# Post-norm transformer block on one core: the last batch's attention in two query blocks, pairwise stack transfers, silu through tanh

## The chip, the core and the metric

One NeuronCore of a Trainium2 chip. The metric is device time in microseconds of one launch. The engines are PE (matmul), DVE (VectorE), ACT (ScalarE), POOL (GpSimd) and SP, which here only issues DMAs. Every engine runs its own list of instructions in order and meets the others only at semaphores.

## What is computed

x is 4 batches x 512 tokens x 128 features, fp32; 16 heads of 8 features; the hidden width is 512.

```python
qkv = einsum('bnd,ed->bne', x, qkv_w) + qkv_b      # per head q, k, v of 8
attn = softmax(q @ k.T * 8**-0.5)                  # 16 heads, 512 x 512
x = layernorm(x + (attn @ v) @ fc_w.T + fc_b + x)
h = silu(tlin(x, w1)) * tlin(x, w2)                # tlin: matmul with a ternary weight, times a scale
h = gelu(tlin(h, h1)); h = gelu(tlin(h, h2))       # exact gelu
x = layernorm(x + tlin(h, w3))
```

## The kernel before

**Orders by hand.** `SP_ORDER`, `PE_ORDER`, `ACT_ORDER`, `DVE_ORDER` and `POOL_ORDER` (L8 to L66) are lists of tokens. `walk` (L264) yields them with a running number, and each engine's loop turns a token into instructions with its waits. In PE_ORDER `S:5` also says in which of the 8 PSUM banks the result goes; `until_free` waits until the bank's last reader is done.

**Attention.** q and k are split in three bf16 parts each (`parts`, tokens `q`, `r`, `mid`, `lo`, `da`, `db`), six slots of part products per head. `spread` and `first_spread` (`zq`, `zk`, L343) copy them by DMA to `stack[0]` (q) and `stack[1]` (k), one DMA of 48 KB per head and side: even heads in partitions 0 to 63, odd heads in 64 to 127. So one bf16 matmul of 64 rows gives exact scores. `S` makes the scores of 128 queries x 512 keys, `s` on DVE takes the negated row maximum (L803). When all `S` of a group (mostly 4 heads) are through, `m` on POOL splits the maxima in three bf16 parts, PE transposes them, ACT copies them to `mT` and `mrow` puts them by two DMAs into three more rows of the stack. `T` repeats the score matmul transposed (128 keys x 512 queries) with the maximum already subtracted, `e` on ACT is the exponential (L654) into one of 16 `prob` buffers, and `P` multiplies four heads' probabilities with V (and a column of ones for the sum), 32 columns of the array for each head. `S` runs some 30 tiles ahead of `T`. After two P groups: `o` (copy to SBUF, transpose), `or`, `om` (reciprocal, normalise), `a` (transpose of the result), `f` (output projection), `l1` with five steps (add, statistics, aggregate, add of eps, result) and POOL's power `p1` between the fourth and the fifth.

**MLP**, in float32r with each activation in a high and a low part. `X` transposes x1, `Xh`/`Xl` split it; `A` and `B` are the two gates, 4 blocks each; `t` and `u` on ACT, `t` on DVE, `u` on POOL form the gate; `h0`/`l0` split it; `H` are the pieces of the hidden layers (4 output blocks x 4 input blocks, two matmuls each, the high and low part), `h` copies, `g` is a gelu over all four blocks, `gh`/`gl` split the result; `W`, `w3`, `Y`, `l2` (with POOL's `p2`), `out`. The weights' low parts are tested for zero once (`L`), and are zero, so each product takes one weight.

**Units.** `UNITS` are what goes through the MLP at once: batches 0, 1, 2 whole (512 columns) and batch 3 as two halves of 256. The attention of batch 3 runs whole, so both halves begin their MLP after the last `P`. For them silu is ACT's Silu (`ws`) and the rest of the gate and all splits are DVE's; up to batch 2's first hidden layer the splits are POOL's. `K` on PE are four filler matmuls of a zero tile.

**Weights.** h1 is loaded at the start, h2 and w3 (`lh`, `l3` in SP_ORDER) behind the stack transfers of batch 0; `wt` transposes them, `wc`/`wl` on POOL split them.

## Time and profile before

| | |
|---|---|
| median of 3 runs | 324.12 us (322.74 to 324.79) |
| span of the profiled execution, first to last instruction | 320.4 us |
| instructions in it | 5569 |
| matmul records, DVE, ACT, POOL instructions | 1804, 516, 433, 227 |
| row maxima on DVE, exponentials on ACT | 256, 256 |
| DMAs `stack<-parts`, 48 KB each | 124 from SP, 4 from ACT |

The profile is one execution. Its span is 3.7 us under the median. "Busy" is the time in which at least one instruction of an engine is under way; matmuls are pipelined, so for PE it is not work. A record's duration holds its latency, so that instructions of one engine start closer together than their durations say.

### The profile page before, as it was taken

The page shows a single profiled execution, that of the slowest core. Times are in us where ns is not written, and L with a number is a line of the kernel's source. Part 1 is how long each engine was busy: PE and PEld are TensorE (multiplying, and loading weights), DVE is VectorE, ACT ScalarE, POOL GpSimd, SP SyncE. Part 2 cuts the span into 40 slices and gives each one's busy share as a digit, 9 for nine tenths or more (in the row PEclk, how much of TensorE's full clock was granted, in tenths as well). Part 3 has the DMA queues.
Part 4 walks back from the last instruction along what each step waited for, and adds up shares of the span by engine and source line. Part 5 has one row for each costly group of instructions (what it writes and reads, how often), then busy time and mean ns, then how long its engine had stood idle before and what let it go on. Part 6 is the DMA issues. An engine that isn't in the chain of part 4 may idle for free.

```text
span 320.4 us, 5569 instructions
## 1 busy us (share of the span) xinstructions
PE 295.8 (92%) x1804; PEld 138.5 (43%) x1804; DVE 244.1 (76%) x516; ACT 234.8 (73%) x433; POOL 148.8 (46%) x227
## 2 busy tenths in 40 slices
PE   8567998999997999999999999999999999999991
PEld 6421132422332344334544233625634353579990
DVE  3959899998989899998996859298684410289883
ACT  3562567999683896898688998697799989447340
POOL 6762038651043793118807778063478913610201
PEclk9985899999999899999999999999999999999996
DMA  5643353313211321212030023310100010000101
...
DMA packets 17830, 13.44 MB, mean 42 GB/s; under 512 B 2551, under 2 KB 16648, under 8 KB 17800
## 3 DMA queue, kind: packets, MB, share of 16 engines
...
## 4 chain that ended last, share of the span: by engine, by line
PE 60%; ACT 11%; DVE 9%; POOL 8%; issue 6%; DMA 4%; SPq 1%; ACTq 1%; POOLq 0%; DVEq 0%
PE bank L445 26%; PE bank L480 11%; PE bank L465 9%; PE bank L456 6%; DVE negmax L803 6%; ACT prob L654 4%; DMA h_nat<-in_L_ffn_h_w_dram 3%; PE bank L420 2%; ACT L654 2%; POOL hT L990 2%; POOL parts L960 2%; PE bank L531 1%; ACT h_nat L729 1%; PE bank L438 1%; PE bank L503 1%
## 5 line engine op out<-in xcount | busy, mean ns | idle before, releaser
L803 DVE TENSOR_REDUCE negmax<-bank 128x1 f32<-128x512 f32 x256 | 160.2, 682 | 23.0 <-PE bank L456 22.5
L654 ACT ACTIVATE prob<-bank 128x512 f32<-128x512 f32 x256 | 136.7, 604 | 29.0 <-PE bank L465 27.4
L480 PE MATMUL bank<-prob,v_sb 128*32 128x512 f32 x512 | 73.0, 608 | 0.4 <-ACT prob L654 0.3
L456 PE MATMUL bank<-stack 61*128 61x512 bf16 x256 | 65.9, 398 | 4.3 <-DMA stack<-parts 2.6
L445 PE MATMUL bank<-act,hT 128*128 128x512 f32 (+1 forms) x320 | 68.3, 359 | 0.1
L465 PE MATMUL bank<-stack 64*128 64x512 bf16 x256 | 61.4, 389 | 2.2 <-DVE negmax L803 1.0
L445 PEld LDWEIGHTS bank<-act,hT 128*128 128x128 f32 x320 | 49.2, 190 | 14.3 <-issue 6.4
L722 ACT ACTIVATE h_nat<-bank,hs_all 128x512 f32<-128x512 f32 (+1 forms) x40 | 22.8, 603 | 22.4 <-PE bank L445 22.4
L456 PEld LDWEIGHTS bank<-stack 61*128 61x128 bf16 x256 | 17.6, 94 | 49.7 <-issue 26.9
L978 POOL CAST mparts<-negmax 128x16 bf16<-128x16 f32 (+1 forms) x17 | 3.7, 219 | 74.3 <-DVE negmax L803 74.3
L465 PEld LDWEIGHTS bank<-stack 64*128 64x128 bf16 x256 | 14.0, 94 | 51.0 <-issue 36.2
L954 POOL TENSOR_TENSOR rstd<-rstd,mhalf 128x4 f32<-128x4 f32 (+1 forms) x10 | 10.1, 1006 | 35.1 <-DVE rstd L784 35.1
L1028 POOL TENSOR_TENSOR act<-h_nat,act 128x512 fp32r<-128x512 f32 x20 | 25.4, 1274 | 1.3
L1023 POOL CAST act<-h_nat 128x512 fp32r<-128x512 f32 x20 | 12.1, 610 | 19.1 <-ACT h_nat L729 19.1
L480 PEld LDWEIGHTS bank<-prob,v_sb 128*32 128x32 f32 x512 | 10.7, 108 | 21.1 <-issue 17.2
L445 PE MATMUL bank<-x1T,w12T 128*128 128x512 f32 (+1 forms) x80 | 18.4, 372 | 0.4 <-DVE x1T L858 0.4
L840 DVE RECIPROCAL rden<-bank 128x32 f32<-128x32 f32 x8 | 2.8, 351 | 18.3 <-PE bank L420 18.3
L1013 POOL TENSOR_TENSOR act<-work,act 128x512 fp32r<-128x512 f32 x12 | 15.2, 1278 | 0.7
L1002 POOL TENSOR_TENSOR work<-work 128x512 f32<-128x512 f32 x12 | 15.2, 1282 | 0.4 <-ACT work L712 0.3
L445 PEld LDWEIGHTS bank<-x1T,w12T 128*128 128x128 f32 x80 | 12.7, 195 | 4.9 <-issue 2.0
L960 POOL COPY parts<-parts 128x512 bf16<-128x512 bf16 x12 | 7.9, 693 | 8.6 <-ACT parts L666 8.6
L427 PE MATMUL bank<-wz 128*128 128x128 bf16 x97 | 9.8, 245 | 1.4 <-DVE wz L752 1.0
(120 smaller groups left out, 343.0 us busy)
## 6 DMA issues: line engine op xcount, KB each, us to landing
stack<-parts SPq DMA_DIRECT2D x124, 48.0 KB
...
h_nat<-in_L_ffn_h_w_dram SPq DMA_DIRECT2D x1, 1024.0 KB, 8.1
work<-in_L_ffn_h_w_dram SPq DMA_DIRECT2D x1, 1024.0 KB, 5.6
...
stack<-mT SPq DMA_DIRECT2D x30, 6.0 KB
```

Source lines behind the costliest of these rows:

```text
L445: mm = nc.tensor.matmul(dst, w, v, start=first and n == 0, stop=last and n == len(pairs) - 1)
L456: nc.tensor.matmul(space("S", n)[:, :], stack[0][half_of(h, MROW), h // 2, qt * P:(qt + 1) * P], stack[1][half_of(h, MROW), h // 2, :], st ...
L465: nc.tensor.matmul(space("T", n)[:, :], stack[1][half_of(h, TR), h // 2, kt * P:(kt + 1) * P], stack[0][half_of(h, TR), h // 2, :], start= ...
L480: last = nc.tensor.matmul(space("P", pfirst)[at:at + VW, :], v_sb[b % 2][:, kt, of:of + VW], prob[:, t % NP, :], start=kt == 0 and slot % ...
L654: nc.scalar.activation(prob[:, n % NP, :], space("T", n)[:, :], ACT.Exp, scale=SCALE).then_inc(emptied("T", n), 1)
L722: nc.scalar.activation(raw[:, k, cols(u)], space(*h_first(u, layer, k))[:, 0:width(u)], ACT.Gelu if direct(u, layer) else ACT.Copy, scale= ...
L803: nc.vector.tensor_reduce(negmax[:, g % 2, col:col + 1], space("S", n)[:, :], AX.X, ALU.max, negate=True).then_inc(emptied("S", n), 1)
L960: nc.gpsimd.tensor_copy(parts[i][:, a, :], parts[i][:, 0, :])
L1002: nc.gpsimd.tensor_tensor(gate[:, k, cols(u)], gate[:, k, cols(u)], up[:, n % 2, cols(u)], ALU.mult).then_inc(gate_ok, 1)
L1013: nc.gpsimd.tensor_tensor(a[1][:, k, cols(u)], gate[:, k, cols(u)], a[0][:, k, cols(u)].bitcast(F32), ALU.subtract).then_inc(lo0, 1)
L1023: nc.gpsimd.tensor_copy(acts[u][layer + 1][0][:, k, cols(u)], raw[:, k, cols(u)]).then_inc(hi_g, 1)
L1028: nc.gpsimd.tensor_tensor(a[1][:, k, cols(u)], raw[:, k, cols(u)], a[0][:, k, cols(u)].bitcast(F32), ALU.subtract).then_inc(lo_g, 1)
```

## The change

- **Units and groups.** The attention of batch 3 is done for queries 0 to 255 and then for 256 to 511 (units 3 and 4), in groups of 8 heads. A `T` tile of them is two matmuls of 256 columns for two key blocks in one bank, and a `P` step is two sets of four matmuls of 256 columns. o, a, f, l1 and the MLP run per unit, so that unit 3's can stand among unit 4's attention in the orders.
- **Stack.** `parts` has eight slots. Slot 6 and 7 hold zeros (q) and ones (k), set once, instead of memsets of the whole stacks. One DMA of 128 rows fills a pair of heads on one side, and one DMA (two in units 3 and 4) brings a group's maxima, now four rows per head. The head order in V and in `om` is plain; v is four, om two smaller instructions instead of two and one.
- **Silu** is tanh on ACT and a product on DVE in all units (`hs12` scales), as it was in batches 0 to 2.
- **Who splits.** POOL now also splits batch 2's second hidden layer, unit 3's gate and unit 3's first hidden layer; DVE splits unit 3's second and all of unit 4's. Unit 3's first hidden layer has the wide gelu, the second and unit 4's have gelus per block.
- **Orders.** All five are new. SP issues `more`, `l3` and the second `lh` ahead of the first stack transfers, ACT issues no DMAs. `K`, `ws` and `wg` are gone.

The core of the diff:

```diff
-lw lh xin vb zq*4 zk*6 zq mrow zq*3 lh l3 xin mrow more xres xin spread mrow spread mrow spread mrow spread mrow spread xres mrow spread mrow spread
-mrow spread mrow*2 spread xres mrow spread mrow spread out spread mrow xres mrow*2 out*4
-"""
+lw lh xin vb
+more l3 lh zq zk*2 zq*2 xin zq*2 zk*3 zq zk*3 mrow zq*2 mrow xres mrow*2 spread*2 xin mrow spread mrow spread mrow xres spread mrow spread mrow spread
+mrow spread mrow*2 xres spread*3 mrow spread mrow*2 xres out mrow*2 out*4"""
...
-H:0 H*3 f:6 H:7 H*3 H:5 H*3 X:4 K:0 X:3 W:1 W A:2 B:0 A:6 B:7 A:5 B:4 A:2 B:3 A:6 B:0 A:5 B:7 A:2 B:4 A:6 B:5 W*2 H:3206 H*4 Y:7 H*5 H:4157 H*9 H:3206
-H*9 H:4157 H*9 W:3 W*3 K:0 W:2 W Y:0 W K:1 W K:0 Y:6
...
+W:0 W T:2 T:7 T:3 T:5 W*2 P*3 Y:4 H:1 o:2 H*3 H:7 H*3 H:3 H a:5 H*2 H:0 H*3 f:6 X:4 H:2 A:5 A:1 A:7 A:3 B:0 B:6 B:4 B:5 H*3 H:1 H*3 H:0 H*3 H:6 H*2
+W:2 H H:7410 H W H W*2 H*6 Y:3 H H:6527 H*9 W:4 W*3 Y:1"""
...
-h e*3 h e g e*5 wg o a*2 h*4 ws t*8 wg w3 h*16 w3*2
+h e h e*2 h m h g o e*3 a e*3 m e*14 t u t*3 w3 u*2 e*4 o u e*8 o a h*3 m h g t u*2 t*3 e*12 u h e u h e*3 m h*2 g o e*16 w3 o a h*4 g t*4 h*4 w3 h*8
+w3"""
...
+s*2 t*4 l2*2 s*3 or om s*2 l2 s*3 or om s*5 l1*5 l2*2 s Xh s Xl s*6 t s*2 t*3 s*4 or om l2*2 or om l2*4 l1*5 Xh Xl t*2 gt*2 h0 l0 t gh gt h0 l0 gl gh
+h0 gh t gl*2 gh gl gt h0 l0*2 gh gl gh*3 gl*3 l2*3 gh gl gh*2 gl gh gl*2 l2*7"""
...
+p1 gl*2 xr u h0 l0 u*3 h0*2 l0 h0 l0*2 m p1 p2 gh*2 gl gh gl gh gl*2 u*2 m u gh*4 gl*4 u h0*3 l0*2 h0 l0*2 p2 p1 gh*2 gl gh*2 gl*3 p2*2"""
...
-    GROUPS = [(0, 0, 2), (0, 2, 2)] + [(b, GH * j, GH) for b in range(B) for j in range(NG) if b or j]
-    UNITS = [(b, 0, NT) for b in range(LAST)] + [(LAST, t0, 2) for t0 in (0, 2)]
+    UNITS = [(0, 0, NT), (1, 0, NT), (2, 0, NT), (3, 0, 2), (3, 2, 2)]
+    NU = len(UNITS)
+    GROUPS = [(0, 0, 2), (0, 2, 2), (0, 4, 4), (0, 8, 4), (0, 12, 4), (1, 0, 4), (1, 4, 4), (1, 8, 4), (1, 12, 4), (2, 0, 4), (2, 4,
+              4), (2, 8, 4), (2, 12, 4), (3, 0, 8), (3, 8, 8), (4, 0, 8), (4, 8, 8)]
+    GATE_DVE = {4}
+    SPLIT0 = [0, 0, 0, 0, 1]
+    SPLIT_G = [(0, 0), (0, 0), (0, 0), (0, 1), (1, 1)]
+    DIRECT = {(3, 1), (4, 0), (4, 1)}
+    INNER_K = {4}
...
+        def spread(eng, i, p, done):
+
+            eng.dma_start(stack[i][:, p, :], parts[i][2 * HD * p:2 * HD * (p + 1), :, :]).then_inc(done, 16)
 
...
-                    for e in range(2):
-                        sp.dma_start(stack[0][TR * e + MROW:TR * e + TR, s0 // 2:(s0 + ns) // 2, :],
-                                     mT[rows * e:rows * (e + 1), 0:P]).then_inc(mrow[n % NG], 16)
+                    each = m_dmas(n)
+                    rows, to = m_rows(n) // each, nt // each
+                    for d in range(each):
+                        sp.dma_start(stack[0][MROW:P:MSTEP, s0 // 2:(s0 + ns) // 2, (t0 + to * d) * P:(t0 + to * (d + 1)) * P],
+                                     mT[rows * d:rows * (d + 1), :]).then_inc(mrow[n % NG], 16)
...
+                    w, each = width(u), N // width(u)
+                    for c in range(each):
+                        kt = each * k + c
+                        last = nc.tensor.matmul(space("T", n)[:, c * w:(c + 1) * w], stack[1][half_of(h), h // 2, kt * P:(kt + 1) * P],
+                                                stack[0][half_of(h), h // 2, cols(u)], start=True, stop=True)
+                    last.then_inc(ps_st, 1)
...
+                    for c in range(each):
+                        for t in range(t0, t0 + nh):
+                            _, k, slot = T_TILES[t]
+                            kt, at, of = each * k + c, VW * (slot % GH), VC * slot
+                            last = nc.tensor.matmul(space("P", pfirst)[at:at + VW, 0:w], v_sb[b % 2][:, kt, of:of + VW],
+                                                    prob[:, t % NP, c * w:(c + 1) * w],
+                                                    start=kt == 0 and slot % (GH * PO) < GH, stop=kt == NT - 1 and slot % (GH * PO) >= GH)
...
-                    if u < LT:
-                        nc.scalar.activation(gate[:, k, cols(u)], space("A", n)[:, 0:width(u)], ACT.Tanh, scale=hs12[:, 0, k:k + 1]).then_inc(ev_w1, 1)
-                    else:
-                        nc.scalar.activation(gate[:, k, cols(u)], space("A", n)[:, 0:width(u)], ACT.Silu, scale=hs[:, 0, k:k + 1]).then_inc(emptied("A", n), 1)
+                    if BEFORE[u]:
+                        until_0(act, lo0, BEFORE[u] - 1, k)
+                    nc.scalar.activation(gate[:, k, cols(u)], space("A", n)[:, 0:width(u)], ACT.Tanh, scale=hs12[:, 0, k:k + 1]).then_inc(ev_w1, 1)
...
-            def k_ones(j):
-                nc.vector.memset(stack[1][:, 2 * j:2 * j + 2, :].rearrange("p h n -> p (h n)").bitcast(F32), TWO_ONES).then_inc(ones, 1)
-
             nc.vector.memset(wz[:, :], 0.0).then_inc(wz_ok, 1)
-            for j in range(NG):
-                k_ones(j)
+            nc.vector.memset(parts[1][:, 6:8, :].rearrange("p m n -> p (m n)").bitcast(F32), TWO_ONES).then_inc(ones, 1)
...
 
-            for j in range(NG):
-                nc.gpsimd.memset(stack[0][:, 2 * j:2 * j + 2, :].rearrange("p h n -> p (h n)").bitcast(F32), 0.0).then_inc(zeros, 1)
+            nc.gpsimd.memset(parts[0][:, 6:8, :].rearrange("p m n -> p (m n)").bitcast(F32), 0.0).then_inc(zeros, 1)
+            nc.gpsimd.memset(mparts[:, :].bitcast(F32), 0.0).then_inc(parts_z, 1)
```

## Rows read from the trace of the kernel before

**Rows 1.** The page, busy time, share and instructions of each engine

```profile
PE 295.8 (92%) x1804; PEld 138.5 (43%) x1804; DVE 244.1 (76%) x516; ACT 234.8 (73%) x433; POOL 148.8 (46%) x227
```

**Rows 2.** Busy by stretch: PE, PEld, DVE, ACT, POOL, then clock, DMA share, GB/s

```profile
20.00:40.00 20.00, 17.22 (x61) 3.44 (x62) 18.46 (x31) 10.27 (x26) 5.63 (x13) 0.66 0.36 64
...
18.70:120.00 101.30, 93.01 (x521) 29.38 (x522) 93.52 (x168) 74.70 (x155) 47.55 (x79) 0.92 0.30 60
120.00:274.80 154.80, 153.27 (x917) 65.33 (x916) 106.49 (x212) 133.09 (x227) 82.02 (x117) 1.00 0.13 25
274.80:320.40 45.60, 37.62 (x284) 33.88 (x280) 32.89 (x116) 18.84 (x40) 7.52 (x8) 0.94 0.05 14
```

**Rows 3.** Groups by line and form: busy us, mean ns, idle before

```profile
L803 DVE TENSOR_REDUCE negmax<-bank 128x1 f32<-128x512 f32 x256 | 160.2, 682 | 23.0 <-PE bank L456 22.5
L722 ACT ACTIVATE h_nat<-bank,hs_all 128x512 f32<-128x512 f32 x24 | 16.5, 688 | 13.4 <-PE bank L445 13.4
L722 ACT ACTIVATE h_nat<-bank,hs_all 128x256 f32<-128x256 f32 x16 | 6.3, 475 | 8.9 <-PE bank L445 8.9
L729 ACT ACTIVATE h_nat<-h_nat 128x2048 f32<-128x2048 f32 x5 | 9.6, 1911 | 0.1
L729 ACT ACT_TABLE_LOAD x5 | 6.4, 1283 | 0.2
L1028 POOL TENSOR_TENSOR act<-h_nat,act 128x512 fp32r<-128x512 f32 x20 | 25.4, 1274 | 1.3
L1023 POOL CAST act<-h_nat 128x512 fp32r<-128x512 f32 x20 | 12.1, 610 | 19.1 <-ACT h_nat L729 19.1
```

**Rows 4.** Timeline of PE: start, duration, then what, with its count

```profile
129.92 1.07 PE L480 MATMUL bank<-prob,v_sb 128*32 128x512 f32 x8
130.91 0.39 PE L456 MATMUL bank<-stack 61*128 61x512 bf16 x2
...
135.62 1.20 PE L445 MATMUL bank<-act,hT 128*128 128x512 f32 x4
136.75 0.39 PE L465 MATMUL bank<-stack 64*128 64x512 bf16 x1
...
292.31 1.09 PE L445 MATMUL bank<-act,w3T 128*128 128x512 f32 x4
293.24 2.56 PE L445 MATMUL bank<-act,hT 128*128 128x256 f32 x20
```

**Rows 5.** Timeline at the start of the tail

```profile
273.77 1.06 PE L480 MATMUL bank<-prob,v_sb 128*32 128x512 f32 x8
...
278.21 0.71 PE L531 MATMUL bank<-fcT,aT 128*128 128x128 f32 x4
...
281.21 0.60 DVE L793 TENSOR_SCALAR x<-res,mv,rstd 128x128 f32<-128x128 f32 x2 [0.81 <-POOL rstd L954]
```

**Rows 6.** Groups of the gate on DVE and of the power on POOL

```profile
L877 DVE SCALAR_TENSOR_TENSOR work<-bank,hs_all,work 128x256 f32<-128x256 f32 x8 | 3.7, 478 | 0.0
L884 DVE CAST act<-work 128x256 fp32r<-128x256 f32 x8 | 2.3, 285 | 0.0
L889 DVE TENSOR_TENSOR act<-work,act 128x256 fp32r<-128x256 f32 x8 | 3.3, 415 | 0.0
L954 POOL TENSOR_TENSOR rstd<-rstd,mhalf 128x4 f32<-128x4 f32 x6 | 7.1, 1190 | 14.0 <-DVE rstd L784 14.0
L954 POOL TENSOR_TENSOR rstd<-rstd,mhalf 128x2 f32<-128x2 f32 x4 | 2.9, 730 | 21.1 <-DVE rstd L784 21.1
```

**Rows 7.** Timeline, the last copy of W3's result

```profile
312.60 0.47 ACT L733 ACTIVATE h_nat<-bank,hs_all 128x256 f32<-128x256 f32 x1 [1.94 <-PE bank L445]
```

**Rows 8.** The chain at the start; a DMA issue, KB and us to landing

```profile
4.78 8.12 DMA h_nat<-in_L_ffn_h_w_dram
...
17.07 3.14 DMA stack<-parts
...
work<-in_L_ffn_h_w_dram SPq DMA_DIRECT2D x1, 1024.0 KB, 5.6
```

514 lines of the change are left out of this document (242 added, 272 removed).

## Prediction

> **What bounds the kernel now.** I read four views: the engines' busy time, the busy time by stage, the timeline of TensorE and the chain and timeline at both ends. No engine is full over the span: PE shows 92%, DVE 76%, ACT 73%, POOL 46% [rows 1]. By stage it looks different, and I cut the run at 18.7, where the first score matmul starts, and at 274.8, where the last probability-times-V step ends [rows 2, 5]:
> - Start, 18.7 us: loads, projections, the first stack transfers.
> - Attention, 256.1 us. Up to 120, DVE is busy 93.5 of 101.3 us; its 256 row maxima alone are 160 us [rows 2, 3]. After 120, PE is busy 153.3 of 154.8 us and DVE only 106.5 [rows 2]. So DVE leads the first part and PE the second.
> - Tail, 45.6 us, 14% of the span, in which nothing is left to overlap with. PE is busy 37.6 us of it: the second hidden layer and W3 of batch 2, then both halves of batch 3 through the whole MLP [rows 2].
>
> PE's busy time overstates its work, since matmuls overlap. I price its stream from starts: a P step of four heads takes 0.99 us; four MLP matmuls of 512 columns take 0.93 us when more of them follow (0.23 each), but 1.13 us when a score or T matmul follows [rows 4]. So a change of the kind of matmul costs 0.1 to 0.2 us; I take 0.1, because P to S shows little of it. Twenty MLP matmuls of 256 columns take 2.56 us, 0.13 each [rows 4]. The Trainium skill (TensorEngine Tiling, Key Properties) says that a change of tiling mode drains the array; the rows agree in that the same four matmuls cost 0.2 us more ahead of a change. By that rule alone the sum would be the same.
>
> **The change, part by part.**
>
> *The tail.* Now only the second half of batch 3 has its attention last. In the tail the PE order holds, before: 40 MLP matmuls of 512 and 176 of 256 columns, 40 x 0.23 + 176 x 0.13 = 32 us. After: 160 of 256 columns (32 H pieces of the first half, its W3, the whole MLP of the second), 160 x 0.13 = 21 us. The new tail is then no longer full of matmuls and its length is a chain, counted from the last P (L):
> - copy of oT, transposes, normalise, attn transpose, aT, output projection: L to L+3.9, as now (273.77+1.06 to 278.92) [rows 5].
> - Layernorm 1 takes 281.81-278.92 = 2.9 us now [rows 5]. After the change DVE has the last step of batch 2's layernorm 2 ahead of it, which waits for POOL's power of the same unit, itself queued behind `h0`/`l0` of the first half. The power over 4 tiles is 1.19 us against 0.73 over 2 [rows 6], and the results of four tiles are twice the work of the two at 281.21, which took 0.60 [rows 5]. I put layernorm 1 at L+5.5 instead of L+3.9, its end at L+8.3. If POOL is early the delay is 0, so the bounds are 0 and 3.
> - Transpose and split of x1: +1.3, A(4,0) at about L+9.7. `H(3,1,0,0)` stands ahead of it on PE and waits for POOL's split of the first half's first layer, which begins after the power at L+7.5; a 512-column split is 0.61+1.27 us [rows 3], a 256-column one I take at half, 0.95. So it is ready near L+9 and hidden, by under 1 us.
> - The gate: four blocks of t (priced as gt, the same form), gt 0.48, h0 0.29, l0 0.42 on DVE [rows 6] = 6.7 us, mixed with four splits of the first half (the same two forms, 0.71 each, 2.8 us): 9.5 us busy, about 8 us start to start, since adjacent ones overlap. `gh(3,1,0)` stands in it behind a chain tanh x4, gelu table load 1.28, h: 0.6 us of waiting. Last `l0` at L+18.8.
> - Two hidden layers, each a last piece on PE (0.25), four gelus of 0.48 [rows 3] and four splits: about 3 us for the first, 3.5 for the second with three steps of another layernorm ahead of its split: L+25.3.
> - W3, its copy, transpose, layernorm 2 and store. Now the last copy starts at 312.60 and the trace ends at 320.4, which is 7.8 us [rows 7]; after, L+25.6+7.8 = L+33.4, less 0.5, because no other unit's result stands ahead on DVE: L+32.9.
> Sum: 32.9 against 45.6, **-12.7 us**. The three table loads of the tail, 1.28 us each [rows 3], one of them for Silu, become a gelu, a tanh and a gelu load; they lie beside DVE's work in both kernels, so silu through tanh itself I cost at 0.48 us per block on DVE (in the sum above) and nothing else.
>
> The clock. PE has nothing to do from the projection (L+3.9) to the transpose of x1 (L+8.3). The filler matmuls K are gone. In 20:40, where the score matmuls wait for DVE, the granted clock was 0.66 on average, so 1.2 GHz for two thirds of it, though PE shows busy for 17.2 us [rows 2]. At that level the tail's 12 us stretch with about 9 us of matmuls would lengthen by up to 7 us. DVE covers part. I take **+1.2**, bounds 0 and 7.
>
> *Attention stage.* What left the tail came here. PE: 264 instead of 224 matmuls of 512 columns (+40 x 0.23 = 9.2), 16 of 256 (+2.0); 28 filler matmuls of 128 columns go (-1.8, at half the price of 256); in the order the kind of matmul changes 214 instead of 255 times (-41 x 0.1 = -4.1); sundry transposes +1.0. Together +6.3 on a stream that I add up to 217 us. T and P of batch 3 are twice as many instructions of half the columns; columns stay, I cost them at nothing (weight loads lie under matmuls: PEld 65 of 155 us [rows 2]); uncovered it would be some 32 x 0.1 = 3 us. ACT: 4 tanh and 4 scaled copies of 256 columns at 0.48 (3.8), four copies of 0.69 (2.8), one wide gelu of 1.91 with two table loads of 1.28 [rows 3], less one load: +9.8, and about +9 start to start. DVE, up to its last maximum: +8 (layernorm and splits of the first half come before it; v and om are more, smaller instructions). POOL: 4 more gate products of 256 columns with their splits and 8 more splits of hidden layers, 4 of them of 512 columns, +17 in all, nearly all here, on an engine busy 129.6 of 256 us [rows 2].
> How much of +6 to +9 shows? PE's stream of 217 us fills 85% of 256.1. The new order puts 16 H pieces of batch 0 (7.3 us) into the part before 120 to 130 us, where DVE leads and PE has room. What is left for the PE-led part is about its old content. So I take **+1**; bounds -4 (the changes of kind alone) and +9 (nothing hidden).
>
> *Start.* The 1 MB load of h2, w3 and the small loads now stand on SP ahead of the first stack transfers. The load of h1 lands at 4.78 + 8.12 = 12.9 [rows 8]; 1 MB alone takes 5.6 us [rows 8], so h2 lands near 19 to 20. The stack transfers are ready to go at about 14 in both kernels (the memsets that go were not what held them), and they took 3.1 us to land [rows 8]. If they land behind h2 the first score matmul is at 21 to 23 instead of 18.7; if not, unchanged. On the other side, the stack's 32 issues per batch become 16, and the mask-row issues are halved, on a queue that holds nothing up later. I take **+2**, bounds -1 and +5. The Trainium skill (DMA: Bandwidth & Descriptors, "Queues, rings and completion order") says that each DMA engine takes its descriptors in the order of the ring; no run yet shows how the stack fares behind h2. By that rule the start would be +3 rather than +2.
>
> **Sum.** 320.4 - 12.7 + 1.2 + 1 + 2 = 311.9 us of span. The profiled execution's span is 3.7 below the median of 324.12 (what lies around it), so **315.6 us**, rounded 315.5.
>
> **Rivals.**
> 1. *The attention stage grows by all that comes into it.* For it: ACT is busy for 81% of it and DVE for 78% [rows 2], ACT's order has more table switches in it, and the slack may be latency, not room. Against: the filler matmuls show room at its end. +9 instead of +1: 323.6, no change. The half clock through the tail (+7 instead of +1.2, 321.4) ends at the same place.
> 2. *POOL turns the sign.* m of a group (four tiny POOL steps) frees the next scores, and four splits of a hidden layer in front of it are 4 x 1.9 = 7.5 us [rows 3]. Now m waits for DVE (POOL idle). After, 28 instead of 20 pairs are POOL's, those of batch 2 too. If two of the m's each wait a whole burst, PE and DVE both stop: +15, 331. It decides from the point where POOL's backlog exceeds the lag of T behind S. Against it: POOL at 129.6 of 256 busy, at most 147 after.
> 3. *The order is simply better.* The stage holds 39 us beyond PE's stream now. If the new order closes a fifth of that, -8 instead of +1: 306.5.
> 4. *The change does nothing at the end*: the chain of the tail is as long as now, since it is latency and not matmuls. Against: PE busy for 37.6 of its 45.6 us [rows 2]. It would be 315.6 + 12.7 - 1.2 = 327.1, and I count it with rival 1.
>
> **How the numbers follow.** The forecast holds with 0.57 (its own range 309 to 321: tail +-3, start +-2, stage -4 to +4), rival 3 with 0.2, rivals 1 and 4 with 0.13, rival 2 with 0.10. About 1% is what a measurement of this kernel tells from no change: 320.9 and 327.4. Faster: 0.57 + 0.2 = 0.77; same 0.13; slower 0.10. The range leaves out 0.1 at each side: 305 to 324.
>
> **What would show it.** The tail from the last P to the end at 33 us (right) or over 38 (wrong); first score matmul at 21; last P at 278; the granted clock in the tail below 0.8 would show the clock's price; ACT idle for PE near zero in 120:270 would show rival 1; m's waits on something else than negmax would show rival 2. What would make it wrong above all: an attention stage that moves by more than 5 us either way, since that is the term with the least ground.

## The result: 3.6% slower, not 2.7% faster

The changed kernel takes **335.83 us** (median of 4 runs, 333.59 to 337.03), the kernel before 324.46 (4 runs) on the same chip: ratio **1.036**, 95% interval 1.030 to 1.041. The prediction was 315.5 us. Here and below, a ratio and its interval leave out executions more than 1.5% above the same kernel's quickest, and a median holds them all; where the granted clock differs between executions (e5, e9, e12, e13, e14, e16), the ratio is therefore that of the quicker ones.

The profiled execution has a span of 335.2 us. It is the slowest of the four (337.03 us, mean clock 0.927; the others 0.942 to 0.946), while the profile of before is a quick one (span 320.4, clock 0.965). So the two profiles differ by 14.8 us and the medians by 11.4, and about 3 us of what follows is the choice of executions. Busy times of the page, and the granted clock in its 40 slices:

```profile
PE 303.1 (90%) x1932; PEld 154.7 (46%) x1932; DVE 244.0 (73%) x515; ACT 237.0 (71%) x438; POOL 163.9 (49%) x253
...
PEclk9789699999999999998999799998999859797897
```

Nearly the same shares as before [rows 1], so the engine totals say little. The stretches do; columns as in [rows 2]:

```profile
20.00:40.00 20.00, 18.25 (x79) 6.69 (x76) 20.00 (x34) 13.30 (x32) 16.46 (x25) 0.83 0.47 98
19.20:120.00 100.80, 96.23 (x549) 34.43 (x549) 96.52 (x176) 75.50 (x151) 47.96 (x85) 0.96 0.33 58
120.00:297.80 177.80, 166.68 (x1128) 84.53 (x1124) 115.66 (x236) 139.99 (x245) 96.39 (x133) 0.93 0.15 26
297.80:335.20 37.40, 26.05 (x182) 23.91 (x178) 22.92 (x83) 12.38 (x26) 8.94 (x15) 0.84 0.06 16
```

The first score matmul starts at 19.2 (18.7 before), the last P step ends at 297.8 (274.8 before), the trace at 335.2. Against the prediction's own span of 311.9:

| us | before | predicted | measured | missed by |
|---|---|---|---|---|
| start | 18.7 | 20.7 | 19.2 | -1.5 |
| attention stage | 256.1 | 257.1 | 278.6 | **+21.5** |
| tail, with its clock | 45.6 | 34.1 | 37.4 | +3.3 |

The miss is 23.3 us of span and 20.3 us of time; nearly all of it is one term, the attention stage. The stretch of [rows 2] in which PE leads was busy for 153.3 of 154.8 us at clock 1.00; now it is busy for 166.7 of 177.8 at 0.93: both idle time and half clock have come in.

To see in what that stage grew, I split TensorE's time from start to start. Each gap counts as work up to the price of its matmul at full clock (0.21 us for 512 columns of a score, 0.23 and 0.12 for 512 and 256 columns of the MLP, 0.1 more at a change of kind); in a stretch at half clock up to as much again counts as clock; the rest is waiting. The sums are measured; the split depends on these prices, and each row is one execution. In the attention stage:

| us | work | half clock | waits | sum |
|---|---|---|---|---|
| before | 223.7 | 6.3 | 26.2 | 256.1 |
| changed | 232.3 | 12.7 | 33.7 | 278.6 |
| e1, POOL waits | 231.6 | 8.9 | 33.0 | 273.4 |
| e12, POOL waits and fillers | 236.7 | 0.0 | 29.6 | 266.3 |

From before to changed: work +8.6 (predicted +6.3, and thought to be nearly all hidden), clock +6.4, waits +7.5. Most of it stands at the end of the stage: up to the 208th exponential the changed kernel is 4.9 us behind (228.9 against 224.0), at the last P 23.0.

### The profile page after: what moved, and what is told of

It reads as the page before. It is cut to its first block, busy times and chain, and to the rows that moved or that the text cites. A ratio compares the mean times of both kernels' runs of the same rounds, so it can differ in the third digit from the quotient of the medians.

```text
span 335.2 us, 5818 instructions
## 1 busy us (share of the span) xinstructions
PE 303.1 (90%) x1932; PEld 154.7 (46%) x1932; DVE 244.0 (73%) x515; ACT 237.0 (71%) x438; POOL 163.9 (49%) x253
## 4 chain that ended last, share of the span: by engine, by line
PE 55%; DVE 16%; ACT 10%; DMA 7%; issue 6%; POOL 2%; SPq 2%; POOLq 0%; ACTq 0%; DVEq 0%
PE bank L465 22%; PE bank L505 13%; DMA stack<-parts 7%; PE bank L476 7%; PE bank L487 7%; DVE negmax L849 6%; ACT prob L713 4%; SPq L363 2%; DVE parts L863 2%; DVE work L922 2%; ACT h_nat L779 1%; DVE y L839 1%; PE bank L529 1%; PE bank L447 1%; PE bank L458 1%
## 5 line engine op out<-in xcount | busy, mean ns | idle before, releaser
L505 PE MATMUL bank<-prob,v_sb 128*32 128x512 f32 (+1 forms) x640 | 72.9, 532 | 0.2
L487 PE MATMUL bank<-stack 64*128 64x512 bf16 (+1 forms) x320 | 62.5, 352 | 2.3 <-DVE attn L900 0.7
L465 PEld LDWEIGHTS bank<-act,hT 128*128 128x128 f32 x320 | 53.4, 200 | 13.7 <-issue 3.7
L476 PEld LDWEIGHTS bank<-stack 64*128 64x128 bf16 x256 | 16.1, 94 | 53.4 <-issue 32.1
L690 POOL CAST act<-h_nat 128x512 fp32r<-128x512 f32 (+1 forms) x28 | 15.7, 584 | 47.6 <-ACT h_nat L779 47.6
L487 PEld LDWEIGHTS bank<-stack 64*128 64x128 bf16 x320 | 18.8, 96 | 35.0 <-issue 16.4
L693 POOL TENSOR_TENSOR act<-h_nat,act 128x512 fp32r<-128x512 f32 (+1 forms) x28 | 33.1, 1200 | 0.3
L505 PEld LDWEIGHTS bank<-prob,v_sb 128*32 128x32 f32 x640 | 16.5, 110 | 26.4 <-issue 18.6
L889 DVE RECIPROCAL rden<-bank 128x32 f32<-128x32 f32 (+1 forms) x10 | 3.1, 313 | 25.8 <-PE bank L546 25.6
L1029 POOL TENSOR_TENSOR work<-work 128x512 f32<-128x512 f32 (+1 forms) x16 | 18.1, 1145 | 4.7 <-ACT work L761 2.7
L675 POOL TENSOR_TENSOR act<-work,act 128x512 fp32r<-128x512 f32 (+1 forms) x16 | 18.1, 1145 | 0.1
L756 ACT ACTIVATE work<-bank,hs 128x512 f32<-128x512 f32 (+1 forms) x20 | 11.2, 609 | 5.5 <-PE bank L465 5.5
L922 DVE SCALAR_TENSOR_TENSOR work<-work,bank 128x512 f32<-128x512 f32 (+1 forms) x20 | 10.9, 572 | 4.0 <-ACT work L756 4.0
```

Source lines behind the costliest of these rows:

```text
L465: mm = nc.tensor.matmul(dst, w, v, start=first and n == 0, stop=last and n == len(pairs) - 1)
L476: nc.tensor.matmul(space("S", n)[:, :], stack[0][half_of(h), h // 2, qt * P:(qt + 1) * P], stack[1][half_of(h), h // 2, :], start=True, st ...
L487: last = nc.tensor.matmul(space("T", n)[:, c * w:(c + 1) * w], stack[1][half_of(h), h // 2, kt * P:(kt + 1) * P], stack[0][half_of(h), h / ...
L505: last = nc.tensor.matmul(space("P", pfirst)[at:at + VW, 0:w], v_sb[b % 2][:, kt, of:of + VW], prob[:, t % NP, c * w:(c + 1) * w], start=k ...
L675: do.tensor_tensor(a[1][:, k, cols(u)], gate[:, k, cols(u)], a[0][:, k, cols(u)].bitcast(F32), ALU.subtract).then_inc(lo0[e], 1)
L690: do.tensor_copy(a[0][:, k, cols(u)], raw[:, k, cols(u)]).then_inc(hi_g[e], 1)
```

## Where TensorE waits

What ended TensorE's waits in the changed kernel (engine, what waited, for whom: us in total, times, longest):

```profile
PE bank L458 <- DVE x L839: 4.8, 2, 3.1
PE bank L440 <- DMA h_nat<-in_L_ffn_h_w_dram: 3.1, 1, 3.1
PE bank L476 <- DMA stack<-parts: 2.9, 4, 1.6
PE bank L546 <- ACT oT L738: 2.0, 3, 1.2
PE bank L476 <- DVE res L817: 1.7, 1, 1.7
```

The first and the last are new (in the kernel before, TensorE waits 0.4 us in all for x). Of the first, 3.1 us stand in the tail, at 306.6, and 1.7 us in the attention stage. The places in the stage in the timeline, at 227 and at 238 us (start, duration, engine, instruction, count, idle before it and what ended it):

```profile
226.92 2.51 POOL L693 TENSOR_TENSOR act<-h_nat,act 128x512 fp32r<-128x512 f32 x2
226.99 3.04 DVE L839 TENSOR_SCALAR x<-res,mv,rstd 128x128 f32<-128x128 f32 x4 [1.14 <-POOL rstd L977]
...
230.08 0.65 PE L458 MATMUL bank<-ident,x 128*128 128x128 f32 x4 [1.66 <-DVE x L839]
...
237.43 0.68 DVE L922 SCALAR_TENSOR_TENSOR work<-work,bank 128x512 f32<-128x512 f32 x1
...
238.02 1.28 POOL L675 TENSOR_TENSOR act<-work,act 128x512 fp32r<-128x512 f32 x1
238.03 4.07 DVE L839 TENSOR_SCALAR y<-res,mv,rstd 128x128 f32<-128x128 f32 x4
...
239.25 2.50 POOL L1029 TENSOR_TENSOR work<-work 128x512 f32<-128x512 f32 x2
...
242.20 0.69 DVE L817 TENSOR_TENSOR res<-bank,x 128x512 f32<-128x512 f32 x1
...
242.95 0.60 PE L476 MATMUL bank<-stack 64*128 64x512 bf16 x3 [1.70 <-DVE res L817]
```

Four result steps of a layernorm, 128 columns each, take 3.04 and 4.07 us. Without a POOL step beside them four take 1.12 (e1, below). Two of the first four and three of the second are long, 1.30 to 1.35 us each, and each of these ends within 0.1 us of the end of a POOL step of 1.27: it looks as if DVE waits for POOL here, and e1 tests it. TensorE needs x at once, and at 241 it waits for the bank that DVE frees right after y. At a third such place, y of unit 1 at 287.4, three of the four steps took 0.64, 1.31 and 1.30 us beside POOL's splits. All over-long DVE steps together are 10.4 us in the changed kernel and 2.9 in the one before. One of those was in the trace of before, and I had not looked at it: a step on 4 columns, 0.16 us elsewhere, that takes 1.19 beside a POOL product:

```profile
248.65 2.52 POOL L1002 TENSOR_TENSOR work<-work 128x512 f32<-128x512 f32 x2
...
250.00 1.19 DVE L784 TENSOR_SCALAR rstd<-mv 128x4 f32<-128x4 f32 x1
```

## Experiments

The theory after the result: (1) POOL, which the change gives more work in this stage (144.4 us busy instead of 129.6; predicted +17), excludes DVE from SBUF and so stretches three layernorms, two of which TensorE waits for; (2) these and other waits let TensorE's clock fall, and the filler matmuls that would keep it up were removed; (3) the matmuls that moved into the stage are not hidden. Rival: the waits and the clock are by-products and the stage simply holds more work.

### POOL and DVE exclude each other: e1, e11, e13

**e1_pool_waits.** POOL waits at three places until DVE has written its results:

```diff
+                PORT = {("gl", 14): (x1_ok, 3), ("l0", 8): (y_ok, 1), ("gl", 20): (y_ok, 2)}
                 for what, n, _ in walk(POOL_ORDER):
+                    if (what, n) in PORT:
+                        pool.wait_ge(*PORT[what, n])
```

> The changed kernel with three waits more on POOL: it holds one of its long steps back until VectorE has written x of unit 2, y of unit 0 and y of unit 1. Theory 1 (POOL and VectorE exclude each other on operands in SBUF): the four result steps of L839 take 0.33 us each again at all three places, where seven of them took 1.30 us; TensorE's waits at 228.2 (1.9 us), 241.0 (2.0 us) and some of 286.3 (1.0 us) shrink, and the time falls by 3 to 7 us, to 329 to 333. Theory 2 (the steps are long but hidden, the loss is the clock and the number of steps): the result steps shrink but the time stays within 1.5 us of 335.8. Theory 3 (the steps are long for a reason of their own): they stay at 1.30 us and the time rises by POOL's delay, 1 to 3 us.

Measured: 331.57 us (4 runs), ratio 1.017 (1.007 to 1.027): 4.3 us below the changed kernel by the medians, 6.1 by the ratios. The two waits of 1.7 us are gone from its trace. Its account above shows only 0.7 us less waiting all the same, since other waits are longer in this execution (4.2 us instead of 2.9 for stack transfers, 2.5 instead of 2.0 for copies of oT), and 3.8 us less half clock.

**e11_two_operands** asks which form of instruction it is. All twelve 512-column products of the gate, `SCALAR_TENSOR_TENSOR` with one operand in a bank, kept their time although eleven ran beside POOL:

```diff
-    nc.vector.tensor_scalar(dst[:, t, :], r[:, t, :], mv[i][:, t, 0:1], rstd[i][:, 1, t:t + 1], ALU.subtract, ALU.mult)
+    nc.vector.scalar_tensor_tensor(dst[:, t, :], r[:, t, :], mv[i][:, t, 0:1], rstd[i][:, 1, t:t + 1].broadcast_to([P, D]), ALU.subtract, ALU.mult)
```

> The changed kernel with the result step of the layer norm in another form, without POOL's waits: (r - mean) * rstd as one SCALAR_TENSOR_TENSOR whose second operand is rstd broadcast from SBUF, instead of a TENSOR_SCALAR. In the changed kernel's trace TENSOR_SCALAR, CAST and COPY with all operands in SBUF were the ones stretched beside a POOL step, while SCALAR_TENSOR_TENSOR with one operand in a bank took 0.68 us each of eleven times beside one. Theory A (what excludes POOL is the fast form of the instruction): the steps take 0.28 to 0.45 us at all places, and the time falls by 3 to 5 us, as with POOL's waits, to 331 or 332. Theory B (two operands in SBUF exclude POOL as well; the Trainium skill, SBUF - State Buffer, says so of a POOL step that reads SBUF): steps of 1.3 us remain at 227, 238 and 287, and the time stays within 1.5 us of 335.8.

Measured: 334.61 us, ratio 1.028 (1.022 to 1.034). The groups of the result steps and of the gate's product, grouped by line and form (busy us, mean ns | idle before), of the changed kernel:

```profile
L839 DVE TENSOR_SCALAR y<-res,mv,rstd 128x128 f32<-128x128 f32 x16 | 9.8, 667 | 2.7 <-POOL rstd L977 2.7
...
L922 DVE SCALAR_TENSOR_TENSOR work<-work,bank 128x512 f32<-128x512 f32 x12 | 7.7, 679 | 2.6 <-ACT work L756 2.6
...
L839 DVE TENSOR_SCALAR x<-res,mv,rstd 128x128 f32<-128x128 f32 x16 | 6.7, 473 | 2.8 <-POOL rstd L977 2.8
```

of e1:

```profile
L839 DVE TENSOR_SCALAR y<-res,mv,rstd 128x128 f32<-128x128 f32 x16 | 5.0, 367 | 2.7 <-POOL rstd L980 2.7
...
L839 DVE TENSOR_SCALAR x<-res,mv,rstd 128x128 f32<-128x128 f32 x16 | 4.7, 356 | 2.8 <-POOL rstd L980 2.8
```

and of e11:

```profile
L839 DVE SCALAR_TENSOR_TENSOR y<-res,mv,rstd 128x128 f32<-128x128 f32 x16 | 10.2, 694 | 2.7 <-POOL rstd L977 2.7
...
L839 DVE SCALAR_TENSOR_TENSOR x<-res,mv,rstd 128x128 f32<-128x128 f32 x16 | 6.7, 473 | 2.8 <-POOL rstd L977 2.8
```

The mean of 16 y steps falls from 667 to 367 ns with POOL's waits, and stays at 694 with two operands in SBUF. So the form TENSOR_SCALAR is not what matters, and a step with one of two operands in a bank escapes. SBUF alone is not what matters either: the statistics step of the layernorm, whose one operand is in SBUF, kept its time in all eight cases beside POOL (0.27 to 0.29 us), four of them here in the changed kernel:

```profile
246.18 2.52 POOL L675 TENSOR_TENSOR act<-work,act 128x512 fp32r<-128x512 f32 x2
...
247.43 0.86 DVE L821 BATCH_NORM_STATS2 stats<-res 128x6 f32<-128x128 f32 x4
```

The Trainium skill says all three (SBUF — State Buffer, "Who interferes with whom"): the second read and write port of DVE is POOL's only one, it is a lock for a whole instruction, and both the fast forms of copy, cast and tensor_scalar and a step with two SBUF inputs ask for it, others not. These runs agree, with 0.33 us alone and 1.3 us behind POOL's 1.27.

**e13_fill_no_waits** is e12 (below, all fillers) without POOL's waits, so that little of the clock is left in the comparison.

> e12_more_fill without POOL's three waits: all fillers, and the exclusion of POOL and VectorE as in the changed kernel. Theory A (the exclusion costs its own length where TensorE waits for it, 1.7 us at 228 and 1.9 us at 241, and the clock the rest): 328 to 330 against e12's 325.9, and the clock falls at 231 in some executions. Theory B (all of the exclusion's price was the clock): within 1 us of 325.9. Theory C (the exclusion carries nearly all, the fillers little): over 331.

Measured: 329.49 us, ratio 1.011 (1.005 to 1.017), against e12's 325.94 and 0.9995 (0.995 to 1.004). Theory A: the exclusion costs about 3.6 us. In e13's trace the two waits stand again, at 1.3 and 2.3 us, and in e12's they are absent. Some clock is in the 3.6 all the same: in e13's profile (the slowest of its four executions, 334.2) TensorE is at half clock for 3.4 us from 243.8, right behind the wait of 2.3, and for 3.4 us from 288.1; e12's profile has no half clock in the stage. In e1, without the fillers, the removal brought 4.3 us; the two prices are not told apart by these intervals.

### The clock: e2, e4, e5, e9, e12, e14, e15

In the changed kernel, what stood in these stretches (columns as above, the clock is third from the end):

```profile
252.00:258.00 6.00, 6.00 (x29) 4.66 (x28) 4.85 (x18) 2.22 (x4) 2.25 (x6) 1.00 0.00 0
258.00:262.00 4.00, 3.31 (x22) 2.33 (x21) 2.88 (x6) 2.99 (x3) 0.30 (x1) 1.00 0.02 6
262.00:265.50 3.50, 2.71 (x12) 0.86 (x11) 3.50 (x7) 3.48 (x8) 2.54 (x4) 1.00 0.00 0
265.50:275.70 10.20, 10.01 (x38) 6.01 (x39) 3.61 (x8) 8.12 (x15) 7.54 (x12) 0.50 0.01 2
275.70:286.00 10.30, 10.30 (x109) 6.75 (x107) 0.00 (x0) 8.07 (x13) 0.32 (x1) 1.00 0.02 4
```

At 258 to 265.5 TensorE waits for the split of x1 and then, short matmul by short matmul, for DVE's row maxima; after that it runs at 1.2 GHz for 10.2 us although it is full. Other stretches at half clock: 33.4 (6.8 us), behind short matmuls that wait 0.2 to 0.3 us each for DVE and ACT, and 156.3, 187.0, 231.3 and 289.4 (3.4 us each) and 306.4 (6.8 us), at or behind a wait of 1.2, 1.6, 1.7, 0.7 and 3.1 us. Not every such wait has one: behind that of 1.7 us at 241 the clock stayed up here, and fell in e13.

**e4_before_no_fillers** takes the 16 `K` tokens out of the kernel before, and nothing else (the expectation's 28 is the number of single matmuls that stood in the attention stage).

> The kernel before without its 28 filler tokens (groups of four matmuls, most in the tail). If the fillers hold the clock up in its tail, the clock falls somewhere behind 275 us, a half-clock stretch of 3 to 14 us appears and the time rises by 1 to 6 us, which would be a part of what the changed kernel, without fillers, gives away. If they do nothing: within 1 us of 324.5, or up to 2 us faster.

Measured: 327.93 us, ratio 1.013 (1.004 to 1.022). The same stretch, before and in e4:

```profile
275.00:300.00 25.00, 24.28 (x172) 21.53 (x170) 19.65 (x67) 13.00 (x25) 4.85 (x6) 1.00 0.01 2
```

```profile
275.00:300.00 25.00, 22.20 (x108) 15.61 (x101) 12.90 (x40) 12.19 (x23) 6.44 (x7) 0.74 0.01 1
```

A stretch of 13.7 us at half clock appears at 274.3. The fillers were worth about 4 us (1 to 7 by the interval), and the change dropped them. Not all of it need be that stretch: the half clock near the first scores, where no filler stood, is longer in e4's profile too (17.1 us against 13.7).

**e2_fillers** puts 30 of them into the changed kernel:

```diff
-T:3 T:4 X:1 S:2
+T:3 T:4 K:1*8 X:1 S:2
-X:4 S:3 S:6 S:1 S:0 S:5 A:7
+X:4 S:3 S:6 S:1 S:0 S:5 K:7*4 A:7
-T:2 o:7 T:7 T:3 T:5
+T:2 o:7 K:3*4 T:7 T:3 T:5
-f:6 X:4 H:2 A:5
+f:6 K:4*14 X:4 H:2 A:5
```

> The changed kernel with 30 groups of four filler matmuls put into the order of TensorE where it waits: 8 ahead of X of unit 2, 4 ahead of the first A of unit 3, 4 at the T behind the last block's attention output, 14 ahead of X of unit 4. Theory A (the half-clock stretches that follow these waits cost 8 to 12 us, and a busy TensorE keeps the clock): the stretches at 231 (3.4 us), 265 (10.2 us), 289 (3.4 us) and 306 (6.8 us) go, the mean clock rises from .93 or .94 to .97 or more, and the time falls by 4 to 9 us. Rival B (the clock falls for what TensorE does in the sparse stretch of S and T at 262 to 266, not for the waits filled here): the one at 265 stays and only 2 to 4 us are won. Rival C (fillers only push real work back): 0 to +3 us.

Measured: 337.89 us, ratio 1.044 (1.037 to 1.052). The clock rose (0.955) and the time did not fall. The prediction had priced a group of four at 0.26 us (28 matmuls at 1.8); it takes 0.46, since each waits for the one before it to leave the bank. Eight groups in its timeline:

```profile
226.49 3.59 PE L448 MATMUL bank<-wz 128*128 128x128 bf16 x32
```

Eight and fourteen groups, 3.7 and 6.4 us, overran the waits of 1.7 and 3.1 us at which they stood. **e5_pool_waits_short_fill** is e1 with 2 groups in place of the 4 and 7 in place of the 14, and none elsewhere.

> e1_pool_waits with 9 groups of filler matmuls, each now counted at the 0.46 us that it took in e2_fillers and not more of them than the wait holds: 2 ahead of the first A of unit 3 (wait 1.07 us), 7 ahead of X of unit 4 (wait 3.39 us). Theory A (the clock is worth having in the tail): no half-clock stretch between 292 and 324 (there was one of 6.8 us at 300.4), the tail shortens from 38.1 by 1.5 to 3 us, 328.5 to 330 against 331.6. Rival (PE is not what sets the tail's end, the chain through VectorE is): the clock stays up and the time stays within 1 us of 331.6.

Measured: 329.21 us over 10 runs (324.91 to 332.38), 1.015 of the kernel before by the medians; the ratio 1.005 (1.001 to 1.010) is that of its five quickest executions. The spread goes with the clock: the three runs at a mean clock of 0.963 took 324.9, 325.3 and 325.5, the six at 0.949 or below 328.5 to 332.4. The tail is 35.3 us instead of e1's 38.1, as Theory A had it. **e9_twice** goes at the thin stretch. No bank is free there for a filler, so matmuls that wait for a reader anyway are simply issued twice:

```diff
-nc.tensor.matmul(space("S", n)[:, :], stack[0][half_of(h), h // 2, qt * P:(qt + 1) * P],
-                 stack[1][half_of(h), h // 2, :], start=True, stop=True).then_inc(ps_s, 1)
+for _ in range(2 if n >= 246 else 1):
+    last = nc.tensor.matmul(space("S", n)[:, :], stack[0][half_of(h), h // 2, qt * P:(qt + 1) * P],
+                            stack[1][half_of(h), h // 2, :], start=True, stop=True)
+last.then_inc(ps_s, 1)
...
-for c in range(each):
+for c in range(each) if not 246 <= n <= 251 else (0, 1, 0, 1):
```

> e5_pool_waits_short_fill with work that is done twice, to the same result, where TensorE waits for VectorE or ScalarE: the last ten score matmuls and six of the last T steps (ten matmuls of 0.21 us and twelve of 0.11 us more, 3.4 us in all, nearly all in gaps of 0.3 to 0.5 us at 255 to 258 and 282 to 285). Theory A (the 10.2 us at half clock from 258 on follow from the thin stretch at 255 to 258, and cost 4 to 5.6 us): the stretch is gone, the row maxima stay 0.6 us apart, and the time falls by 3 to 5 us from 329.2 (fast cases of e5 at 325 to 321 or 322). Rival (the clock falls there all the same, or the extra matmuls delay TensorE): no change to +3 us.

Measured: 329.01 us (322.72 to 330.22). In its trace the stretch is at full clock:

```profile
252.00:262.00 10.00, 9.31 (x57) 5.66 (x58) 7.88 (x20) 7.52 (x12) 4.13 (x6) 1.00 0.01 2
262.00:272.00 10.00, 9.76 (x61) 6.04 (x60) 3.80 (x8) 9.77 (x20) 7.34 (x12) 1.00 0.01 2
```

but the median did not move from e5's: in this profile the clock fell at 156, 187 and 282 instead. Three of the four executions took 328.0 to 330.2; the fourth, at clock 0.971, took 322.7, less than any of e5's ten. With four executions that is no verdict on e9 by itself. **e12_more_fill** adds groups at the two waits behind which it had fallen at 156 and 187:

```diff
-m:1 o:6 S:7
+m:1 K:6*4 o:6 S:7
-H:0 H T:7 S:6 S:1
+H:0 H T:7 K:6*4 S:6 S:1
```

> e9_twice with 8 filler groups more (4 ahead of the transpose of the second attention output of unit 1, which waits 1.9 us for ScalarE's copy at 153, and 4 ahead of the first score matmul of unit 3, which waits 1.8 us for its stack transfer at 184), 0.46 us each. Theory A (waits of TensorE of over 1 us are what lets the clock fall, wherever they stand): no half-clock stretch between 40 and 275 us in any execution, mean clock .97 and more, time 322 to 326 (e9_twice had one execution at 322.7, the others at 328 to 330). Rival (the fall has other causes): the stretches at 156 and 187 stay in some executions and the median stays at 328 to 330.

Measured: **325.94 us** over 10 runs (321.7 to 328.75), ratio 0.9995 (0.995 to 1.004; 1.003 by the medians): as fast as the kernel before. Stage and tail of e1 and then of e12:

```profile
19.30:292.60 273.30, 259.27 (x1673) 117.43 (x1673) 204.24 (x407) 215.27 (x396) 143.75 (x215) 0.96 0.22 38
292.60:330.70 38.10, 25.68 (x182) 23.53 (x178) 22.94 (x83) 12.40 (x26) 8.95 (x15) 0.83 0.06 16
```

```profile
19.70:285.90 266.20, 255.88 (x1735) 117.12 (x1735) 205.21 (x411) 215.03 (x396) 144.98 (x217) 1.00 0.22 39
285.90:322.70 36.80, 27.52 (x210) 24.55 (x206) 22.95 (x83) 12.39 (x26) 8.94 (x15) 0.87 0.06 16
```

The stage is at clock 1.00 and 7 us shorter, with 62 more matmuls in it. From e1 to e12 the fillers and doubled matmuls win 5.6 us, from the changed kernel to e13 6.3 (8 by the ratios). With both causes mended e12 is still 10.4 us above the prediction, and its stage, 266.2 us, is 9.1 above the predicted 257.1: that rest is the moved work as far as it shows, and small waits.

**e14_start_fill** and **e15_before_start_fill** do the same for the start, in e12 (`K:0*7` ahead of `wt:0`, `K:1*2` ahead of `hs:1`) and in the kernel before (`K:0*7` ahead of `wt:0`, `K:5*3` and `K:4*2` ahead of its first two `S`).

> e12_more_fill with nine filler groups more at the start: 7 ahead of the transpose that waits 3.3 us for the load of h1, 2 ahead of the one that waits 1.4 us for the small scales. Theory A (half clock at 13 to 20 us makes the eleven or so transposes and projections there late, and with them the first score): first score at 18 to 19 instead of 19.7, 1 to 2 us less in all, 324 to 325. Rival (the first score waits for its stack transfer anyway): within 1 us of 325.9.

> The kernel before with twelve filler groups more at its start: 7 ahead of the transpose that waits 3.6 us for h1's load, 3 and 2 ahead of the first two score matmuls, which wait 1.5 and 1.3 us. If the half clock at 21 to 35 costs time there: the stretch is gone and the time falls by 2 to 5 us, to 319 to 322. If VectorE leads that stretch (a row maximum each 0.6 us, beside which a matmul at half clock still fits): the clock rises and the time stays within 1 us of 324.2.

Measured: e14 326.12 us, ratio 1.003 (0.999 to 1.007); e15 **322.93** us over 10 runs, ratio 0.995 (0.992 to 0.998). In e14 the half clock ahead of the first score is gone and nothing is won: the first score (20.1) waits for its stack transfer. In e15 I was wrong about the place: the stretch of 13.7 us stays in its profile, only later (24.1). But that profile is the slowest of its ten executions (325.5 us, clock 0.959). Seven of the ten took 322.3 to 323.1 at a clock of 0.966 to 0.972, where the kernel before had 0.950 to 0.966 in the 17 executions listed beside e16. So the gain of half a per cent goes with a higher clock; where in the kernel it is higher, no trace shows. It is the only version here that is faster than the kernel before.

### Is the moved work hidden? e6, e7, e16

**e7_half_h** leaves out the low part's product of 16 H pieces (second hidden layer of unit 2, which the change moved into the stage); **e16_more_fill_half_h** does so in e12.

```diff
-    [a[:, kk, cols(u)] for a in acts[layer]], kk == 0, kk == NK - 1)
+    [a[:, kk, cols(u)] for a in (acts[layer][:1] if (u, layer) == (2, 1) else acts[layer])], kk == 0, kk == NK - 1)
```

> The changed kernel with half the work of 16 H pieces left out, those of the second hidden layer of unit 2, which the change moved from the tail into the attention stage (of each piece the product with the low part of the activations: 16 matmuls of 512 columns, 0.23 us each, 3.6 us of TensorE's stream; no order and no wait changes). If the stream of TensorE sets the stage, as its accounts of before and after say (nothing of the moved work is hidden): 3 to 5 us less than 335.8, more where they ran at half clock. If the stage is set by latencies of other engines (the prediction's view that such work hides there): less than 1.5 us.

> e12_more_fill with the same 16 matmuls of 512 columns left out as in e7_half_h (the products with the low part in the second hidden layer of unit 2): 3.6 us of TensorE's stream in the attention stage. If the stream sets that stage (nothing of what was moved there hides): 321.9 to 323 against 325.9, ratio to the kernel before .988 to .993. If latency sets it: 325 to 326.

Measured: e7 332.27 us, ratio 1.022 (1.015 to 1.030), 3.6 below the changed kernel. e16 324.8 us over 12 runs, ratio 1.003 (0.999 to 1.006), which is between 1.1 below (medians) and 1 above (ratios) e12. The two disagree. In e16's profile the work of the stage's last part is 2.9 us less, 1.4 of it comes back as half clock (at 279) and 0.7 as other waits: TensorE with less to do waits more and its clock falls. Its whole stage is no shorter than e12's (267.5 against 266.2), with half clock at 20, 37 and 279 where e12's had none, and the mean clock of its twelve executions is lower (median 0.967 against 0.972). So the claim that the whole stream shows is not borne out: with less to do, TensorE lost some of the gain to the clock. How much of the moved work hides stays open.

**e6_scores_earlier** moves two scores of unit 4 out of the thin stretch into the H block ahead of it (PE: `H*2 S:3 S:6 H:2 H*3 X:4 S:1`, DVE: `s*3 Xh Xl s*5`), on top of e1.

> e1_pool_waits with two score matmuls of unit 4 moved from behind X of unit 3 into the block of H pieces ahead of it, and their two row maxima on VectorE ahead of the split of x1. VectorE is idle or nearly so at 255 to 259 and full at 260 to 270, where TensorE waits 2.5 us for row maxima. Theory A (this sparse stretch costs its waits and starts the half-clock stretch at 263 to 270): the waits for row maxima behind 256 fall from 1.7 us to under 0.7, the half-clock stretch goes, and the time falls by 2 to 5 us below e1's 331.6. Rival (the stretch is filled elsewhere): waits move by under 1 us and the time stays within 1 us of 331.6; or the split of x1 comes later and costs 1 us more.

Measured: 331.35 us, ratio 1.020 (1.013 to 1.027), e1's time. The half-clock stretch at 263 stays and the waits behind the last scores went from 8.7 to 9.2 us. The rival held: two tiles are not what makes the order thin there.

### The other parts of the change: e3, e8, e10

**e3_head_per_transfer**: a transfer per head of the eight-slot stack.

```diff
-            eng.dma_start(stack[i][:, p, :], parts[i][2 * HD * p:2 * HD * (p + 1), :, :]).then_inc(done, 16)
+            for e in range(2):
+                at = HD * (2 * p + e)
+                eng.dma_start(stack[i][SR * e:SR * e + SR, p, :], parts[i][at:at + HD, :, :]).then_inc(done, 16)
...
```

> The changed kernel with one part undone: the stacks are filled with a transfer for each head (64 KB, 32 of them in a batch) instead of one for a pair (128 KB, 16). If the pair per transfer is a gain: the first score matmul moves from 19.3 us to 20 or 21, the waits of TensorE for the spread queue (1 to 2 us at 62, 116 and 183) grow, and the time rises by 1 to 5 us. If the large transfers are what makes it late there (a transfer of twice the size lands later): the waits shrink and the time falls by 1 to 3 us. If the stacks are off the path: within 1 us.

Measured: **356.7 us**, ratio 1.102 (1.092 to 1.113), 21 us slower than the changed kernel and far outside what I had allowed. TensorE's waits in e3:

```profile
PE bank L478 <- DMA stack<-parts: 9.2, 5, 3.1
PE bank L489 <- DMA stack<-mT: 7.1, 2, 5.4
```

The first was 2.9 us with pairs; the second was nothing: a row of maxima that T needs stands on SP behind twice as many spreads. With orders made for pairs, transfers of half the size cost the path. It does not say what pairs would bring to the kernel before, whose orders were made for single heads (its two waits for stack transfers sum to 2.6 us) and whose transfers are of 48 KB.

**e10_h2_later** puts the load of h2 behind the first stack transfers, on top of e5 (SP: `lh` moves from behind `l3` to behind the last `zk`).

> e5_pool_waits_short_fill with the 1 MB load of h2 moved on the queue from ahead of the first stack transfers to behind them (16 for the first batch are issued before it). Theory A (the prediction's start term: the stack's first rows land behind h2): the first score matmul moves from 20.2 to 18 to 19 us and the time falls by 1 to 2 us. Rival 1 (the same transfers share the DMA engines anyway, and h2's transposes now come late and stop TensorE near 25 us): the first score is earlier, the end is not, within 1 us. Rival 2 (h2 was never in the way): first score within 0.3 us of 20.2.

Measured: 340.26 us, ratio 1.054 (1.047 to 1.061), 11 us slower than e5 by the medians. The first score came at 17.8 instead of 20.2, as Theory A said of it, and then TensorE stood still:

```profile
18.98 0.71 PE L441 MATMUL bank<-ident,h_nat 128*128 128x128 f32 x5
32.18 1.09 PE L441 MATMUL bank<-ident,work 128*128 128x128 f32 x4 [12.49 <-DMA work<-in_L_ffn_h_w_dram]
```

The load is 2 us in the way of the first score, and its place is right: the order behind it asks for h2 at 19.

**e8_silu_tail** gives unit 4's gate back to ACT's Silu, without the product on DVE (`ACT.Silu` of A with the scale `hs`, `t` on DVE left out, the scale of the second product `hs` instead of `hs12`).

> The changed kernel with one part undone: the gate of the last unit by Silu on ScalarE instead of tanh on ScalarE and a product with the pre-activation on VectorE. Takes four steps of 0.41 us off VectorE in the tail's chain. By the prediction (silu through tanh costs its steps on VectorE and nothing else, no table load more or less): the tail shortens by 0.5 to 1.6 us. Rival (the two functions differ in table loads or the steps on VectorE are hidden): within 0.5 us of 335.8, or up to 1.3 us longer if one more table load stands in the chain.

Measured: 336.55 us, ratio 1.033 (1.024 to 1.041). Its tail is 36.6 us against 37.4, within what the prediction implies, but the time shows no difference (336.55 against 335.83, and the intervals overlap): not settled.

## Why the prediction was wrong, by its own steps

**Start, +2 (bounds -1, 5).** Right in kind. h2's load holds the first score up by 2.4 us (e10), and the measured first score was 0.5 to 3.5 us later than the 18.7 of before, by execution (19.2 to 22.2 in twelve profiles of kernels with this start; with the start of before 18.7 and, in e4, 20.2). The profiled execution of the changed kernel was the earliest. Of the 3.7 us that the prediction adds for what lies around the span, 1.8 do (337.03 against 335.2); the other 1.9 were that the profiled execution of before was quicker than its median. The sum is not hurt by it.

**Tail, -12.7 and clock +1.2.** The mechanism was right and gave the largest part of what was foreseen: 37.4 us against 45.6, and 34.1 predicted. With L = 297.8, in the profile after:

```profile
302.93 0.61 PE L559 MATMUL bank<-fcT,aT 128*128 128x128 f32 x4
...
303.57 0.42 DVE L813 TENSOR_TENSOR res<-bank,res 128x256 f32<-128x256 f32 x1 [0.24 <-PE bank L559]
...
305.81 0.78 DVE L839 TENSOR_SCALAR x<-res,mv,rstd 128x128 f32<-128x128 f32 x2 [0.81 <-POOL rstd L977]
...
306.64 0.69 PE L458 MATMUL bank<-ident,x 128*128 128x128 f32 x2 [3.11 <-DVE x L839]
...
318.50 0.75 DVE L675 TENSOR_TENSOR act<-work,act 128x256 fp32r<-128x256 f32 x2
...
328.02 0.47 ACT L783 ACTIVATE h_nat<-bank,hs_all 128x256 f32<-128x256 f32 x1 [1.89 <-PE bank L465]
```

Layernorm 1 starts at L+5.8 (predicted 5.5) and ends at L+8.8 (8.3). The last `l0` ends at L+21.5 (18.8), the last copy starts at L+30.2 (25.6). So the gate was 2.2 and the two hidden layers with W3 2.0 us too cheap. From 306.4 to 313.3 TensorE was at 1.2 GHz, behind the 3.1 us wait shown. Without such a stretch the tail takes 35.3 in e5 (e1, the same but for the fillers: 38.1), so the clock costs 2 to 3 us here (taken: 1.2, bounds 0 and 7), and some 2.4 us are latency of the chain.

**Attention stage, +1 (bounds -4, 9): the step that failed.** It measured +22.5, outside its own bounds. The prediction read the kernel before rightly (stream, +6.3 priced against 8.6 counted) and then failed three times:
- It took slack for room: "PE's stream of 217 us fills 85% of 256.1". The remaining 15% were waits of order and latency and half clock (26.2 and 6.3 us by the account, beside a stream of 223.7), and they did not shrink when work came in. Of the 8.6 us at most some hid: taking 3.6 of them out brought 3.6 in one pair of kernels and about nothing in the other.
- It had no price at all for two engines in one memory. DVE's +8 and POOL's +17 (measured from first score to last P: +12 and +15) were added up as if side by side. The exclusion cost 3.6 us with the clock mostly held (e12, e13), 4.3 by the medians or 6.1 by the ratios with what it does to the clock (e1).
- It priced the loss of the fillers in the tail only, 1.8 us in favour of their removal in the stage and 1.2 against in the tail. The half clock in the attention stage cost 6.4 us more than before; fillers at the new waits brought 5.6 and 6.3 us. The trace of before had the warning, the clock of 0.66 in 20:40 [rows 2], and it was used for the tail alone.
These are 8.6 of work less what hides, 6.4 of clock and 7.5 of waits, of which 3.4 are the two that the exclusion made. The other 4 us or so are small ones (for stack transfers, for copies of oT, for exponentials), and none was tested by itself. Fillers, doubled matmuls and POOL's waits together (e12) took 9.9 us off the 11.4 by which the medians differ; the other half of the 20.3 us between prediction and result is argued from the accounts and not shown by a run.

**The rivals.** Rival 2 had the sign, the size (331) and the engine, POOL, but not the mechanism: TensorE waited less for it than before (none of its listed waits is for `mparts`; before, one of 1.1 us was). Rival 1, +9 by all that comes in, was the nearest to what the work did; had it added the half clock, which it named beside it, it would have had the sign. It was given 0.13.

**What would have made it right.** The prediction said that the term with the least ground was the stage. Its range should then have held the sum of that term's upper bound and the clock's, 315.5 + 8 + 6 = 329.5, not one or the other. That is still 6.3 us short of 335.8. What is missing is the exclusion, the small waits and the 2.4 us of latency in the tail.
